# Scores of a key tile added in place to those of the tile two back

## The reference

```python
q = x @ Wq; k = context @ Wk; v = context @ Wv
sim = jnp.einsum('bhid,bhjd->bhij', q, k) * SCALE
attn = jax.nn.softmax(sim, axis=-1)
out = jnp.einsum('bhij,bhjd->bhid', attn, v)
return out.transpose(0, 2, 1, 3).reshape(B, Nq, INNER_DIM) @ Wo + bo
```

## Time and profile before

| | |
|---|---|
| median of three runs | 4308.6 us |
| profiled execution, its own time | 4298.41 us |
| its span | 4296.6 us |
| granted TensorE clock, mean share of full speed | 0.961 |
| busy PE, DVE, ACT, POOL | 94%, 62%, 42%, 66% |
| `a0`, with its lead-in and end | about 20 to 445 us |
| `c0` | 455 to 2604 us |
| `c1` | 3010 to 4145 us |

### The profile page before, as it was taken

How to read it: one execution, slowest core, us unless ns; L and a number is a source line. 1 busy time by engine, 2 the same in 40 slices (tenths; PEclk the granted TensorE clock), 3 DMA queues, 4 the chain that set the end, 5 groups by cost and what they waited for, 6 DMA issues and landing times. The chain is left out here.

```text
span 4296.6 us, 71788 instructions
## 1 busy us (share of the span) xinstructions
PE 4020.1 (94%) x26404; PEld 2141.9 (50%) x26404; DVE 2685.1 (62%) x3375; ACT 1813.3 (42%) x2105; POOL 2825.2 (66%) x1350
## 2 busy tenths in 40 slices
PE   6999699999999999999999997889899999999969
PEld 3444355554545555555555544633355554555537
DVE  5766767667676676766667622387666666667432
ACT  2444144444444444444444442256244444444433
POOL 3667187878887787877878891000077888878940
PEclk9999899999999999999999998989599999999979
DMA  1000000000000000000000000100000000000001
GB/s 36 6 6 2 5 2 2 2 2 2 2 2 3 2 2 2 2 3 2 2 1 1 2 1 27 35 1 1 4 2 2 2 2 2 2 1 2 1 13 32
DMA packets 25454, 23.92 MB, mean 6 GB/s; under 512 B 6321, under 2 KB 19106, under 8 KB 25122
## 3 DMA queue, kind: packets, MB, share of 16 engines
q1 hardware_dynamic: 23666, 17.05, 1.4%
q10 hardware_dynamic: 1456, 2.46, 0.2%
HBM read 18.97 MB, written 0.52 MB: 5 GB/s over the span
## 5 line engine op out<-in xcount | busy, mean ns | idle before, releaser
L404 POOL TENSOR_TENSOR c_SUM<-c_SUM,c_PR 128x896 f32<-128x896 f32 (+1 forms) x1176 | 2482.9, 2111 | 452.6 <-ACT c_PR L473 360.3
L569 DVE TENSOR_REDUCE c_MX<-c_XB 128x2 f32<-128x1024 f32 (+2 forms) x1156 | 1391.5, 1204 | 849.5 <-PE c_XB L735 848.9
L473 ACT ACTIVATE c_PR<-c_S 128x1024 f32<-128x1024 f32 (+1 forms) x1224 | 1192.9, 1023 | 1628.6 <-PE c_S L769 1553.0
L785 PE MATMUL c_O<-c_PR,c_V 128*64 128x512 f32 (+1 forms) x4896 | 1179.9, 600 | 1.3 <-ACT c_PR L473 1.3
L785 PEld LDWEIGHTS c_O<-c_PR,c_V 128*64 128x64 f32 (+1 forms) x4896 | 316.4, 136 | 542.2 <-issue 382.4
L769 PE MATMUL c_S<-c_SH,c_ONE 64*128 64x512 f32 x2448 | 486.4, 392 | 0.0
L735 PE MATMUL c_XB<-c_KHM,c_QH 64*128 64x512 f32 x1632 | 371.8, 449 | 26.4 <-DVE c_MX L569 20.2
L769 PE MATMUL c_S<-c_QH,c_KHM 64*128 64x512 f32 x1728 | 350.2, 401 | 0.1
L769 PE MATMUL c_S<-c_QH,c_KLM 64*128 64x512 f32 x1728 | 346.0, 396 | 0.0
L769 PE MATMUL c_S<-c_QL,c_KHM 64*128 64x512 f32 x1728 | 345.9, 395 | 0.0
L735 PEld LDWEIGHTS c_XB<-c_KHM,c_QH 64*128 64x128 f32 x1632 | 155.5, 186 | 378.8 <-DVE c_MX L569 206.7
(11 more groups left out here) (264 smaller groups left out, 4541.4 us busy)
## 6 DMA issues: line engine op xcount, KB each, us to landing
f_W<-in_L_w SPq DMA_DIRECT2D x34, 256.0 KB, 2.7
CTX<-in_ctx ACTq DMA_DIRECT2D x12, 192.0 KB, 4.4
c_WQ<-in_L_xattn_Wq SPq DMA_DIRECT2D x12, 64.0 KB, 1.9
c_WO<-in_L_xattn_Wo SPq DMA_DIRECT2D x12, 64.0 KB, 1.9
c_WK<-in_L_xattn_Wk SPq DMA_DIRECT2D x12, 48.0 KB, 1.8
c_WV<-in_L_xattn_Wv SPq DMA_DIRECT2D x12, 48.0 KB, 1.8
X<-in_x SPq DMA_DIRECT2D x1, 512.0 KB, 6.4
a_WQ<-in_L_attn_Wq SPq DMA_DIRECT2D x8, 64.0 KB, 1.9
```

What stands on the lines that cost most here:

```text
L404: pool.tensor_tensor(out[0:kp], out[0:kp], tile[0:kp], ALU.add).then_inc(summed, 1)
L473: act.activation(PR[0:kp, u % BUFS, :, :].rearrange("p h q -> p (h q)"), S[u % 2][0:kp, :], ACT.Exp)\
L569: dve.tensor_reduce(MX[:, q:q + tiles, :, column], bank[:].rearrange("p (h k) -> p h k", h=2) [:, :, 0:tiles * m].rearrange("p h (q k) -> ...
L785: last = pe.matmul(O[ROWS[h], :], V[pair.par][0:kp, t, ROWS[h]], PR[0:kp, u % BUFS, h, :], start=t == 0, stop=t == TILES - 1)
```

## The change

The scores of a tile are no longer made from nothing. For all but four tiles of a half (`whole`: two at the head of each of two chains; in `a0` the first two), the bank still holds the scores of the tile two back, less the shift, and three steps with the difference of the two tiles' keys are added to them. The shift step is left out in these tiles. The keys' high and low parts are now those of the difference, `KD`; the maxima take the keys themselves, rounded, from `KX`.

A K job is made in more parts. ScalarE copies the projected keys to `KX` and their last half or both halves to `K32`, VectorE writes `KD` in two instructions; in the next group ScalarE makes the high part (`high_part`), and VectorE the low part (`low_part`). Values lie in `VM` (one buffer) and `VA` (two), the two-buffered parts of keys and values are smaller, `SPLIT` in `c` is 416, and the side jobs have other places: ten V jobs move to half 1.

```diff
-        self.split = HALF - 64 if wide else HALF
+        self.split = HALF - 96 if wide else HALF
...
-        self.alt = self.chunks - 4 if wide else 0
+        self.alt = self.chunks - 2 if wide else 0
+        self.v_alt = self.chunks - 3 if wide else 0
+        self.whole = {t for c in (0, self.alt) for t in (4 * c, 4 * c + 1)}
...
+            self.division = [2, 2]
+            ends = {(2, 0): "D", (4, 1): "Y", (final, 0): "M"}
+            self.side = [{at: (kind, 1 - half) for at, kind in ends.items()} for half in range(2)]
+            self.side[0][7, 0] = ("Q", 0)
+            for i, c in enumerate(range(self.v_alt, self.chunks)):
+                self.side[0][10 + 3 * i, 0] = ("V", c)
+            self.side[0][final - 1, 0] = ("K", self.alt)
+            self.side[1][0, 0] = ("K", self.alt + 1)
+            self.side[1][1, 0] = ("K", 0)
+            for c in range(1, self.alt):
+                self.side[1][2 * c + 2, 0] = ("K", c)
+            for c in range(self.v_alt):
+                self.side[1][2 * c + 5, 0] = ("V", c)
+            self.side[1][final - 1, 0] = ("Q", 1)
...
-                        act.activation(kh[:, at:at + m], SIDE[:, 0:m], ACT.Copy).then_inc(side_act, 1)
+                        act.activation(KX[:, c * CHUNK:c * CHUNK + m], SIDE[:, 0:m], ACT.Copy)
+                        parts = min(m // (2 * P), 2)
+                        act.activation(K32[:, 0:staged(pair, job) * (parts - 1) + 1:staged(pair, job), :],
+                                       SIDE[:, 0:parts * 2 * P].rearrange("p (b k) -> p b k", k=2 * P), ACT.Copy)                           .then_inc(side_act, 1)
...
+                def high_part(pair, job):
...
+                    act.wait_ge(side_free, number(pair, job, False) + 1)
+                    act.activation(kh[:, at:at + m], KD[:, 0:m], ACT.Copy).then_inc(k_high, 1)
...
-                        dve.tensor_tensor(kl[:, at:at + m], SIDE[:, 0:m], kh[:, at:at + m].bitcast(F32), ALU.subtract)\
+                        if 4 * c in plan.whole:
+                            dve.tensor_copy(KD[:, two], SIDE[:, two])
+                        else:
+                            dve.tensor_tensor(KD[:, two], SIDE[:, two], K32[:, 3 - here, :], ALU.subtract)
+                        dve.tensor_tensor(KD[:, rest], SIDE[:, rest], K32[:, 0, 0:m - 2 * P], ALU.subtract)\
...
+                def low_part(pair, job):
...
+                    dve.wait_ge(k_high, keys_made(pair, job))
+                    dve.tensor_tensor(kl[:, at:at + m], KD[:, 0:m], kh[:, at:at + m].bitcast(F32), ALU.subtract)\
+                       .then_inc(k_low, 1)
...
-                            last = pe.matmul(out, qh[ROWS[h], (q + t) * P:(q + t + 1) * P],
-                                             kh[ROWS[h], at + first:at + first + m], start=True, stop=True)
+                            k = c * CHUNK + first
+                            last = pe.matmul(out, qh[ROWS[h], (q + t) * P:(q + t + 1) * P], KX[ROWS[h], k:k + m],
+                                             start=True, stop=True)
...
-                    terms.append((ONE[:], SH[half][:]))
+                    if t in plan.whole:
+                        terms.append((ONE[:], SH[half][:]))
...
-                                             start=i == 0, stop=i == len(terms) - 1)
+                                             start=i == 0 and t in plan.whole, stop=i == len(terms) - 1,
+                                             skip_group_check=t not in plan.whole)
```

More of the change, by code:

```diff
@@ L291, in k_at, with v_at, differences_before @@
             return KHM, KLM, c * CHUNK
+        def v_at(par, first, tiles):
+            if first < V_ALT:
+                return VM[:, first:first + tiles, :]
+            return VA[par][:, first - V_ALT:first - V_ALT + tiles, :]
+        def differences_before(half, group):
+            at = [(half, group - 1, k) for k in range(3)] if group else [(1 - half, GROUPS - 1, k) for k in range(3)]
+            jobs = [plan.side[h].get((g, k)) for h, g, k in at]
+            jobs = [job for job in jobs if job is not None and job[0] == "K"]
+            assert len(jobs) <= 1 and (group or not jobs)
+            return jobs
         def q_at(par, half):
@@ L481, in _ @@
                         take_v(job, pair_at(0), O).then_inc(v_taken, 1)
+                    elif kind == "low":
+                        high_part(None, ("K", job))
                 def period(pair, end):
@@ L487, in period @@
                                 probabilities(pair, half, t)
+                            if not end:
+                                for job in differences_before(half, group):
+                                    high_part(pair, job)
                             for job in side_jobs(half, group, 0, end) + side_jobs(half, group, 1, end):
@@ L611, in _ @@
                         maximum(job, lead_bank(job), plan.maxima[0][job])
+                    elif kind == "low":
+                        low_part(None, ("K", job))
                     elif kind == "side":
@@ L636, in period @@
                                 normalise(pair, 1 - half, end)
+                            if not end:
+                                for job in differences_before(half, group):
+                                    low_part(pair, job)
                             for job in side_jobs(half, group, 0, end):
@@ L750, in scores @@
                     if t == 0:
+                        if half == 0:
+                            pe.wait_ge(k_low, CHUNKS * (pair.p + 1))
                         if half:
```

86 lines of the change are left out of this document (52 added, 34 removed).

## The result

| | median us | lowest to highest | runs |
|---|---|---|---|
| before, on the same chip | 4308.24 | 4293.22 to 4312.14 | 4 |
| after | 4392.12 | 4369.96 to 4394.06 | 4 |

The changed kernel takes 1.019 of the time (95% interval 1.0149 to 1.023), 84 us more. The forecast was 4368 with a range of 4230 to 4430. The profiled execution took 4390.58 us, of which 4388.8 are its span, 92.2 more than the span before. Executions of one kernel spread with the clock that they are granted: 25 of the kernel before, beside e1, took 4281.0 to 4324.3 us at a mean of 0.970 to 0.948 of full speed.

What follows compares the result with a forecast made beforehand. TensorE was taken to bind most groups, VectorE the fifth groups and half ends. Terms +23 - 16 + 27 + 12 + 15 = +61 on 4298.4 gave 4359; the runs' median lies 10 higher: 4368 us, range 4230 to 4430.

Steps and rivals of the forecast that it cites:

- The plain group: Two-tile group in `c`: 4.38 to 4.13 us, 0.22 of the 0.46 saved lost to bank wait and weight load.
- The fifth group: Every fifth group in `c`, which also reduces `FIVES`: VectorE's chain takes 5.42 us; +4.2 per pair.
- A pair of `c`: Plain groups -9.0, fifth groups +4.2, uncovered places +2.8, half ends +4.3: +2.3 us per pair, ten pairs +23.
- the steps: Steps removed in tiles of `c` not in `whole`: 0.25 us gained in each of 36 groups, -9.0 per pair.
- the key jobs: Key copies, `KD`, `high_part` and `low_part` in `c`: mostly hidden in VectorE's idle time; uncovered places cost +2.8 per pair.
- The term of `a0`: Seven pairs of `a0`: +3.9 us each, from `low_part` and key jobs without cover; +27 in all.
- The lead-in of `c0`: Before the groups of `c0`, VectorE binds; `low_part` and longer `KD` add 0.75 us to each of 13 chunks: +10.
- its clock term: Longer stalls bring one more clock dip in ten of the half ends, at 1.5 us each: +15.
- 1, TensorE keeps pace: Whole kernel: bank's wait costs nothing, 0.46 us back per group, `low_part` finds gaps, columns cost less; 4209 us, chance 0.2.
- 2, key jobs hidden: Whole kernel: key jobs hide, half of `a0`'s cost too, and the clock does nothing; 4313 us, chance 0.15.
- 3, dips after stalls: Fifth groups: each 1.3 us TensorE idle followed by a clock dip, +130; 4500 us, chance 0.08.
- 4, GpSimd binds: Plain groups held at 4.30 us by GpSimd's two additions at a pitch of 2.15, +61; 4430 us, chance 0.05.

Runs made afterwards that it cites:

- e1: The kernel before, only the shift step left out in the tiles where the change omits it (part of the computation missing); 4226.36 us, ratio 0.981.
- e6: The changed kernel, each maximum over 512 keys reading only 448 of them; 4269.04 us, ratio 0.9918 to the kernel before.
- e3: The changed kernel with 448 columns on GpSimd as before, instead of 416; 4320.89 us, ratio 1.0053 to the kernel before.
- e4: The changed kernel with `low_part` replaced by a one-input copy of `KD`, its subtraction left out; 4293.88 us, ratio 0.9975 to the kernel before.
- e5: The changed kernel with `a0` run by the attention of before; 4337.82 us, ratio 1.007 to the kernel before.
- e8: Changed `c` with 448 columns, `a0` of before, key differences written in place in `SIDE`, some jobs moved; 4261.57 us, ratio 0.9888 to the kernel before.
- e10: The kernel before with VectorE's order changed at the ends of halves, lead-in as it was; 4298.6 us, ratio 0.9984.
- e7: The changed kernel with `a0` run by the attention of before and `SPLIT` 448; 4279.67 us, ratio 0.9933 to the kernel before.
- e9: e8 with VectorE's order changed at half ends and, in the lead-in, the low part ahead of the value copy; 4238.41 us, ratio 0.985.

## Why the prediction came out

**Right.** The plain group (4.13, bank wait 0.11, load 0.11), confirmed from the other side by e6. The fifth group, 5.34 for 5.42, with `FIVES` 1.87 for 1.90, `TWOS` 0.56 for 0.60 and `SUM` 2.19 for 2.25. The additions, 1.99 for 1.96. The last halves, -14.2 for -16; TensorE's wait there is 10.26 us, 11.07 before.

A pair of `c` was put at +2.3. The 22 halves took 17.8 + 3.7 = 21.5 more, which is +2.0 per pair. By parts, over `c0` and `c1`, measured and in brackets as predicted: the steps -9.0, from e1 against before (-10.5: -9.0 in the 36 groups and -1.5 inside the fifth ones); the columns +7.6, from after against e3 (+7.2); the key jobs +3.3, from e3 against e1 (+5.4).

**The term of `a0`: the clock behind the stalls was missing from it.** The prediction had +3.9 for a pair, and a pair became 5.7 longer (halves of 26.22 and 23.47 to 25.73 and 29.65). Its `low_part` at the end of half 0, 0.69 behind 0.9 of waiting, is 1.59 in the rows, as priced. The one behind the reciprocals was put at 1.7 and takes 2.63, up to 2.65. In e4 these two take 0.69 and 0.63, and a pair of `a0` is 25.76 + 25.04 = 50.80 us, 1.1 longer than before; the 2.9 us of waits on top would make +4.0, about what was forecast. The other 1.7 are the price of the one stretch at the lower level in that pair, which the prediction had for half ends of `c` and not for `a0`. So by this estimate `low_part` was 0.9 too cheap in one place, terms beside it were as much too dear, and the +16.5 that the stage missed by are the clock's. e5 puts 43 us on `a0`, and e4 gives 37 of them back by this one operation, the stretches at the lower level among them.

GpSimd's additions there are 2.43 us each, and GpSimd has idle time of 3 us and more between pairs of them. `low_part` does not fall into it: the one at 257.86 starts 0.30 us behind the start of an addition that ends at 259.94, and ends 0.55 behind that end.

By the Trainium skill ("SBUF — State Buffer", section "SBUF: two separate sides") such an operation and one of GpSimd that reads SBUF take turns, each holding the port for its whole length. The rows agree: 1.24 and 1.93 us with both inputs in SBUF, 0.68 with one input in the same places (e4), and 0.68 with one of the two in PSUM (e8, at another place in the group). They also show the other turn, an addition that waits for VectorE (last section).

In `c` the same wait cost 39.0 + 15.8 us by e4, 5.0 per pair of the 11. The prediction had about 5.4 for all that the key jobs do there, and took the waits only where a place has no cover; they came at more places than that, 0.55 us in the mean of 132 operations. Since the key jobs' net cost was 3.3, the rest of their new form and of the side jobs' new places would give back 1.7 per pair, if the two can be subtracted (e4 has 416 columns, e1 and e3 448), which I had not seen; which of them does was not tried apart. So the sum for `c` is right partly by luck: the steps were put 1.5 per pair too high, and the key jobs 2.1 too dear.

**The lead-in of `c0`: right at a clock that did not come.** The prediction had VectorE bind it and add 0.75 per chunk, +10. At full clock, which e5 had for the first chunks, the rows show that: 5.79 us for 5.12. In the kernel after, TensorE stayed at the lower clock and bound the lead-in, as it did in e1 with the old instructions (86.4); of the +13, 11 go with the clock and 2 with the new instructions. That the number is near 10 is luck. `c1`'s lead-in, +5, is 3 of the clock (86.3 in e1) and 2 of the change.

**What was not in it.** The clock was expected to cost 15 at half ends of `c`. It cost nothing there: the 15 halves of `c0` had 0.99 of it before and after. It cost 20.4 + 11 + 3 = 34 in code that did not change, and about 17 in `a0`. The 20.4 and the 3 stand in e10 as well, with the code of before in those stages, and one kernel's own executions spread by more, so they are taken as chance; for the 11 this is open. The medians differ by 84, the profiles by 92. Taken out of the 92, the 34 leave 58, where the prediction without its clock term had 46; the 12 between are `a0`'s +16.5 and the lead-ins' -6, with small ends. So the total came near partly by chance. The change's own loss did not: e4 shows that with a `low_part` that does not wait the change is even, and e7 that with `a0` left as before and the old columns in `c` it gains.

**Rivals.** 1, TensorE keeps pace, is refuted by the plain group (4.13, not 3.92). 2, key jobs hidden, by e4. 3, dips after stalls, did not happen in the fifth groups of `c0` that it was made for (0.99 of the clock), but its mechanism did happen in `a0`. 4, GpSimd binds: the groups are 4.13, not 4.30. Where `low_part`'s waits and the new columns are taken away and `a0` is left alone, e8 and e9 come to 4262 and 4238, still above rival 1's 4209.

## What to carry to other kernels

Before taking steps from the busiest engine, follow the next engine's chain through one period: here 0.25 of 0.46 us came back, and in `a0` 2.9 us of waits on VectorE at places without cover cost a pair 4.6 us, the clock counted. Price an operation of VectorE with both inputs in SBUF, beside a GpSimd that adds from SBUF, by where in the addition it starts: here it ended 0.55 us behind the addition's end, up to 2.65 us for 0.69. Keeping one input in PSUM, with new places for some jobs, gave 38 us in `c`, and holding that bank longer cost 19 of them in the lead-ins. And look at the clock, and at stages that no edit touches, before giving a difference of 20 us to the edit.

## What the runs showed that was not expected

- The normalisation `c_OT` by `RDEN`, which the change does not touch, took 0.78 us on average before (its median is in the earlier trace rows), 2.05 after and 1.78 in e1, where only TensorE's steps had changed. The groups by form, before and e1:

```profile
L533 DVE TENSOR_TENSOR c_OT<-c_OT,c_RDEN 128x512 f32<-128x512 f32 x22 | 17.1, 776 | 0.1
```

```profile
L533 DVE TENSOR_TENSOR c_OT<-c_OT,c_RDEN 128x512 f32<-128x512 f32 x22 | 39.1, 1779 | 0.1
```

  Both its inputs are in SBUF, and its length goes by where its start falls. Before, 20 of the 22 start with no addition of GpSimd running or in its last 0.2 us; after, all 22 start while one runs, 20 of them in its first 0.6 us. Two places in e1, with GpSimd's two additions beside each in one row:

```profile
1180.55 4.28 POOL L404 TENSOR_TENSOR c_SUM<-c_SUM,c_PR 128x896 f32<-128x896 f32 x2 [0.67 <-ACT c_PR L473]
1182.74 2.63 DVE L533 TENSOR_TENSOR c_OT<-c_OT,c_RDEN 128x512 f32<-128x512 f32 x1
```

```profile
1048.62 4.82 POOL L404 TENSOR_TENSOR c_SUM<-c_SUM,c_PR 128x896 f32<-128x896 f32 x2 [0.39 <-ACT c_PR L473]
1050.78 0.67 DVE L533 TENSOR_TENSOR c_OT<-c_OT,c_RDEN 128x512 f32<-128x512 f32 x1
```

  At 1182.74 the addition was there 0.03 us earlier, and VectorE's operation ends 0.54 behind it. At 1050.78 both start together, VectorE's takes its 0.67, and the addition 2.66 for 2.11. The 22 at 1.27 more are 28 us of VectorE after.
- TensorE's clock in a lead-in can take either of two courses with the same instructions: 1.2 GHz for all of 86 us, with PE busy 81.59 of 86.44 us, or 0.89 of the full grant on average, 75.3 us, as the windows of before and e1 show.

  By the Trainium skill ("TensorE: Matmul & The Clock Gate", section "Part 1: The HAM clock gate") sustained matmul activity lifts the clock; here a stretch with PE busy for all of its 6.11 us stayed at 0.50, and so did the whole of e1's lead-in. What decides between the two was not found.
